# Order of the dt, q and z projections at the start of a block in a fused Mamba, attention and expert-FFN kernel

## The reference

```python
# layer 1, Mamba: DIN 1024 channels, N 16 states, R 32
x, z = split(layernorm(x0) @ in_proj_w)           # 512 -> 2 x 1024
xc = silu(conv4(x)); ssm = xc @ x_proj_w.T         # 1024 -> 32 + 16 + 16
dt = softplus(rmsnorm(ssm[:32]) @ dt_proj_w.T + dt_bias)
h[t] = exp(dt * A) * h[t-1] + dt * B[t] * xc       # a scan for each state
y = (sum_n h * C + D * xc) * silu(z); x1 = x0 + y @ out_proj_w.T
# layer 2, attention over ctx: 32 heads of 128, 8 key/value heads, rotary
q = layernorm(x1) @ Wq; k = ctx @ Wk; v = ctx @ Wv
x2 = x1 + softmax(mask(rope(q) rope(k).T / sqrt(128))) v @ Wo
# layer 3: a router picks 16 of 64 rank-8 experts
x3 = x2 + ffn(layernorm(x2))
```

## Time and profile before

| | us |
|---|---|
| median of 3 runs | 2348.61 |
| lowest, highest | 2341.81, 2349.77 |
| the profiled execution, its own time | 2350.73 |
| the span in its trace | 2349.1 |
| PE busy in it | 2086.0 |
| DVE busy in it | 1762.5 |
| ACT busy in it | 1003.9 |

### The profile page before, as it was taken

How to read it: one execution, slowest core, us unless ns; L and a number is a source line. 1 busy time by engine, 2 the same in 40 slices (tenths; PEclk the granted TensorE clock), 3 DMA queues, 4 the chain that set the end, 5 groups by cost and what they waited for, 6 DMA issues and landing times.

```text
span 2349.1 us, 26708 instructions
## 1 busy us (share of the span) xinstructions
PE 2086.0 (89%) x8268; PEld 1192.0 (51%) x8272; DVE 1762.5 (75%) x1735; ACT 1003.9 (43%) x2549; POOL 701.3 (30%) x492
## 2 busy tenths in 40 slices
PE   6877887898999988998999989998999989799988
PEld 2333454345555543445556544345556544477774
DVE  4499994459999996259999996259999994456553
ACT  2544440265555532155545541255545540233331
POOL 0289992401111112401111111501111110456550
PEclk9788999889999999989999999989999999799999
DMA  2579895527888873435888874525887874332210
GB/s 63 165 178 230 210 215 169 146 95 175 176 182 196 184 180 101 154 117 135 186 190 179 186 166 119 186 91 136 190 190 181 188 166 117 103 99 90 86 59 18
DMA packets 117810, 352.12 MB, mean 150 GB/s; under 512 B 14016, under 2 KB 14144, under 8 KB 115296
## 3 DMA queue, kind: packets, MB, share of 16 engines
q0 software_dynamic: 40704, 146.82, 32.3%
q1 hardware_dynamic: 70112, 191.68, 26.6%
q10 hardware_dynamic: 6912, 12.59, 1.4%
HBM read 197.68 MB, written 23.33 MB: 94 GB/s over the span
## 4 chain that ended last, share of the span: by engine, by line
DVE 34%; PE 27%; DMA 17%; issue 14%; ACT 3%; POOL 2%; DVEq 1%; PEldq 1%; SPq 0%; POOLq 0%; PEld 0%; ACTq 0%
DMA xc<-hs 15%; DVE hs L1254 11%; DVE hs L1431 4%; PE acc L1753 4%; PE acc L1631 3%; DVE hs L1261 3%; DVE hs L1245 2%; PE pq L1684 2%; PE acc L1837 2%; PE pq L1714 2%; PE pq L1921 2%; PE pk L1921 2%; PE acc L1766 1%; DVE pzsc L1311 1%; DVE qr L1291 1%
## 5 line engine op out<-in xcount | busy, mean ns | idle before, releaser
L768 POOL DMA_DIRECT2D xc<-hs x192 | 164.1, 860 | 1116.3 <-DVE hs L1261 1095.9
L1254 DVE TENSOR_TENSOR_SCAN hs<-dA,hs 128x1024 f32<-128x1024 f32 x192 | 428.7, 2274 | 0.0
L988 ACT ACTIVATE dA<-dt,aneg 128x504 f32<-128x504 f32 x384 | 253.6, 707 | 320.0 <-DVE hs L1254 319.8
L1684 PE MATMUL pq<-qT,wa 128*128 128x512 f32 x768 | 354.1, 615 | 15.1 <-DVE pzsc L1311 14.9
L1766 PE MATMUL acc<-wb,oT 128*128 128x512 f32 x768 | 352.2, 603 | 3.6 <-ACT oT L976 3.6
L1261 DVE TENSOR_TENSOR hs<-hs,bc 128x1024 f32<-128x1024 f32 x256 | 307.6, 1203 | 2.2
L953 ACT ACTIVATE pr<-pzsc,mx 128x64 f32<-128x64 f32 x512 | 170.8, 335 | 245.1 <-DVE mx L1317 245.1
L1245 DVE TENSOR_TENSOR hs<-u,bc 128x1024 f32<-128x1024 f32 x192 | 227.5, 1217 | 26.6 <-DMA xc<-hs 21.0
L1631 PE MATMUL acc<-xnT,wa 128*128 128x512 f32 x512 | 234.4, 612 | 14.3 <-DMA wa<-in_wx 3.9
L1684 PEld LDWEIGHTS pq<-qT,wa 128*128 128x128 f32 x768 | 146.4, 196 | 189.3 <-issue 177.2
L1766 PEld LDWEIGHTS acc<-wb,oT 128*128 128x128 f32 x768 | 141.2, 193 | 148.0 <-issue 143.9
(11 more groups left out here) (255 smaller groups left out, 3379.2 us busy)
## 6 DMA issues: line engine op xcount, KB each, us to landing
xc<-hs POOLq DMA_DIRECT2D x240, 512.0 KB, 7.0
bc<-bc_rows SPq DMA_DIRECT2D x64, 512.0 KB, 7.5
wa<-in_wq SPq DMA_DIRECT2D x64, 512.0 KB, 10.2
wb<-in_wo SPq DMA_DIRECT2D x64, 512.0 KB, 7.0
wa<-in_wx SPq DMA_DIRECT2D x16, 512.0 KB, 7.0
wa<-in_wz SPq DMA_DIRECT2D x16, 512.0 KB, 3.8
wb<-in_ow SPq DMA_DIRECT2D x16, 512.0 KB, 6.3
wv<-in_wv SPq DMA_DIRECT2D x26, 256.0 KB, 13.1
```

The costliest lines, as they stand in the source:

```text
L768: G.dma_start(xc[:, 2 * c:2 * c + 2, :], hs[:, c, :].rearrange("p (d t) -> p d t", t=T), accum_op=ALU.add).then_inc(s_y[c], 16)
L988: ins = S.activation(to[:, :, 1:SEQ], dt[:, s, :].rearrange("p (b t) -> p b t", t=SEQ)[:, :, 1:SEQ], ACT.Exp, scale=aneg[:, s, bass.ds(jj ...
L1254: V.tensor_tensor_scan(out=hs[:, c, :], data0=dA[:, c % 2, :], data1=hs[:, c, :], initial=0.0, op0=ALU.mult, op1=ALU.add).then_inc(scd.sem, 1)
L1684: ins = M.matmul(pq[:, h, :], wa4(p)[:, k, h * P:(h + 1) * P], qT[:, k, :], start=(k == 0), stop=(k == KE - 1))
```

## The change

It concerns the steady stages alone (`mamba and attn`).

- PE: dt is projected before q of pair 0. Of the four loads of z, z0 is projected between q 0 and scores 0, z1 between q 1 and step 0, and z2 and z3 (tiles 4 to 7) behind the whole of step 0, ahead of the zeros.
- ACT: exp and ln of softplus stand ahead of the exponentials of pair 0. Silu of z tiles 4 to 7 (`last_silu_z`) moves behind step 0.
- DVE: softplus chunk 0 stands between rope 0 and mask 0, chunk 1 between the maximum and the inverse sum of pair 0, chunks 2 and 3 behind rope 1. The wait for `y0r` ahead of step 0 goes.
- SP: the loads into `wa` follow PE's new order, q0, z0 | q1, z1, q2, z2, z3 | q3 ...; the loads z2 and z3 and q2 are issued behind those of xa, xr and xm. Step 0 issues no q load of its own.

```diff
@@ SP
-                    for n in range(2):
-                        load_wa(i, at_z + n, a["wz"][n])
+                    if attn:
+                        load_wa(i, 2, a["wq"][1])
+                        load_wa(i, 3, a["wz"][1])
...
+                if mamba and attn:
+                    load_wa(i, 4, a["wq"][2])
+                    for n in range(2, W_DT):
+                        load_wa(i, 3 + n, a["wz"][n])
...
@@ ACT
+                    if mamba and isinstance(jj, int) and jj == 0 and p == 0:
+                        last_silu_z()
...
@@ DVE
-                    for part in (mask_scores, max_scores, invert_sum, probs):
-                        part(0, 0)
+                    if mamba:
+                        softplus(i, ch, [0])
+                    mask_scores(0, 0)
+                    max_scores(0, 0)
+                    if mamba:
+                        softplus(i, ch, [1])
+                    invert_sum(0, 0)
+                    probs(0, 0)
                     rope_q(0, 1)
                 if mamba:
-                    softplus(i, ch)
+                    softplus(i, ch, [2, 3] if attn else range(NCH))
...
@@ PE
+                if attn:
+                    eng.wait_ge(qTr.sem, qTr.upto(blk, KE - 1))
+                    project_q(0, 0)
+                    free_wa(0, 0)
+                if mamba:
+                    eng.wait_ge(dtv.sem, dtv.upto(i, DT_TILES - 1))
+                if mamba and attn:
+                    project_z([0])
+                elif mamba:
+                    project_z(range(W_DT))
                 if attn:
                     scores(0, 0)
                     eng.wait_ge(srd.sem, srd.upto(blk, 0))
                     project_q(0, 1)
                     free_wa(0, 1)
...
+                if mamba and attn:
+                    project_z([1])
...
                     step(0, 0, False, first=True)
                     if mamba:
+                        project_z([2, 3])
                         eng.wait_ge(szr.sem, szr.upto(i, DT_TILES - 1))
```

More of the change, by code:

```diff
@@ L513, in one @@
                         eng.dma_start(bc[:, n, :, :], scr[i, :, n, :].partition_broadcast(P)).then_inc(s_bc[n], 16)
-                    for n in range(2):
-                        load_wa(i, at_z + n, a["wz"][n])
+                    if attn:
+                        load_wa(i, 2, a["wq"][1])
+                        load_wa(i, 3, a["wz"][1])
+                    else:
+                        for n in range(2):
+                            load_wa(i, at_z + n, a["wz"][n])
                     if attn:
@@ L586, in step @@
                         if not tail:
-                            load_wa_j(i, z_uses + 2, jj, p, a["wq"][jj * 2 + (2 + p)])
+                            if not (mamba and isinstance(jj, int) and jj == 0 and p == 0):
+                                load_wa_j(i, z_uses + 2, jj, p, a["wq"][jj * 2 + (2 + p)])
                             if p == 0 and mamba:
@@ L679, in one @@
                 if mamba:
-                    for n in range(2):
-                        load_wa(i + 1, n, a["wq"][n])
+                    load_wa(i + 1, 0, a["wq"][0])
+                    load_wa(i + 1, 1, a["wz"][0] if nxt else a["wq"][1])
                     load_wb(i + 1, 0, a["wo"][0])
@@ L1038, in one @@
                                      bias=chan[:, 1, s:s + 1]).then_inc(dtv.sem, 1)
-                if attn:
+                if attn and not mamba:
                     exps(0, 0)
-                    if not mamba:
-                        swap_q(0, 1)
+                    swap_q(0, 1)
                 if mamba:
@@ L1051, in one @@
                                      ACT.Ln, bias=1.0).then_inc(spl.sem, 1)
+                    if attn:
+                        exps(0, 0)
                     eng.wait_ge(yr.sem, yr.upto(i, -1))
@@ L1070, in one @@
                         S.activation(silu_z(s), acc[:, s % 4, :], ACT.Silu).then_inc(szr.sem, 1)
+                if mamba and not attn:
+                    last_silu_z()
                 def read_unit(at, what, b, g):
@@ L1219, in ssm_rows, with softplus @@
                                        op0=ALU.mult, op1=ALU.mult).then_inc(sstr.sem, 1)
-            def softplus(i, ch):
-                for c in range(NCH):
+            def softplus(i, ch, chunks):
+                for c in chunks:
                     two = slice(2 * c, 2 * c + 2)
@@ L1622, in wa4, with project_in @@
                 return wa[:, p, :].rearrange("p (k c) -> p k c", k=KE)
-            def project_in(b, loaded, banks, free, done):
-                for s in range(DT_TILES):
+            def project_in(b, loaded, banks, free, done, tiles=range(DT_TILES), slot=None):
+                for s in tiles:
                     if s % 2 == 0:
@@ L1629, in project_in @@
                     free(s)
+                    at = slot(s // 2) if slot else (s // 2) % 2
                     for k in range(KE):
-                        ins = M.matmul(banks(s % 4), wa4((s // 2) % 2)[:, k, (s % 2) * P:(s % 2 + 1) * P],
+                        ins = M.matmul(banks(s % 4), wa4(at)[:, k, (s % 2) * P:(s % 2 + 1) * P],
                                        xnT[:, k, :], start=(k == 0), stop=(k == KE - 1))
@@ L1679, in project_q @@
                         return
-                    z_loads = W_DT // 2 if o >= 2 else 0
-                    eng.wait_ge(s_wa[p], (wa_half(i) + (o // 2 + 1 + z_loads) + jj) * 16)
+                    if isinstance(jj, int) and jj == 0:
+                        at = [0, 2, 4, 7][o]
+                        p = at % 2
+                        use_wa(at)
+                    else:
+                        eng.wait_ge(s_wa[p], (wa_half(i) + (o // 2 + 1 + W_DT // 2) + jj) * 16)
                     for h in range(2):
@@ L1838, in one, with free_z, project_z @@
                                  stop=True).then_inc(dtd.sem, 1)
+                def free_z(s):
+                    if s >= 4:
+                        eng.wait_ge(szr.sem, szr.upto(i, s - 4))
+                def project_z(loads):
+                    place = [1, 3, 5, 6] if attn else [at_z + n for n in range(W_DT)]
+                    project_in(i, lambda n: use_wa(place[n]), lambda b: acc[:, b, :], free_z, inz,
+                               range(2 * loads[0], 2 * loads[-1] + 2), lambda n: place[n] % 2)
+                if attn:
+                    eng.wait_ge(qTr.sem, qTr.upto(blk, KE - 1))
[5 more added lines that the diff above has]
+                    project_z([0])
+                elif mamba:
+                    project_z(range(W_DT))
                 if attn:
```

11 lines of the change are left out of this document (1 added, 10 removed).

## The result

| | before | after |
|---|---|---|
| median, us | 2345.58 (4 runs) | 2365.41 (4 runs) |
| lowest, highest | 2341.81, 2349.77 | 2363.02, 2368.13 |
| ratio, 95% interval | | 1.0084, [1.006, 1.0109] |
| span in the trace | 2349.1 | 2363.4 |

The changed kernel is slower by 19.8 us. The chain that ended last, by engine (part 4 of the page of the changed kernel), answers to the earlier trace rows: PE now leads it and DVE follows.

A forecast was written before the change was run, and what follows sets the result against it. DVE is full once step 0 runs, but PE is the nearer limit at mask 2: 10.7 us later less 1.9 given back is 8.8 per stage, 26.4 over three, 2348.61 to 2375 us; 8-in-10 range 2350 to 2391.

The forecast's parts named there:

- dt first: On PE ahead of q 0: 1.9 us lost waiting for ssmT, then dt itself takes 10.5 us.
- The clock: On PE behind dt: q 0 slow at 9.7 us, q 1 7.1, scores 0 at full clock, a gain of 2.9.
- The gain on DVE: On DVE up to mask 1: softplus moved into the waits brings mask 1 7.6 us earlier.
- PE's gap and z behind q 2: On PE before mask 2: 13.9 us without work but values, then q 2, z2, z3; DVE idle some 18 us.
- The load of z3: On SP's queue behind q 2: landing takes 10.2 us, low end 3.8, so z3 lands 2.9 us late for PE.
- B's part: Rival, costs come out low: z3 lands within 3.8 us, q 0 at full clock, q 2 at 8.7; 2355, chance 0.15.
- The mask behind the scores: On DVE at mask 2: the mask starts 0.7 us after scores 2 end on PE.
- silu and zeros: Behind z3: four silus on ACT take 2.07 us uncovered, then PE's four zeros take 1.1 us.
- Given back: On DVE in the step behind mask 2: a 1.9 us wait for an accumulating DMA falls away.
- Rival C: Faster: the 7.6 us that DVE is early at mask 1 carry through mask 2; 2326 at full gain, chance 0.11.
- D: Rival, heavier: q 2 at half clock throughout, 14.1 us not 9.7, another 4.4 per stage; 2388, chance 0.12.

The follow-up runs named there:

- q_first: The changed kernel with q of pair 0 ahead of dt on PE again, all else as changed: 2362.09 us, ratio 1.0085 to the kernel before.
- warm_gap_long: The changed kernel with products of zeros in PE's gap, 24 ahead of values 0 and 25 behind: 2363.1 us, ratio 1.0077 to the kernel before.
- z_ahead: The changed kernel with z2 and z3, their silus and loads, back ahead of step 0: 2333.21 us, ratio 0.9958 to the kernel before.
- z_in_gap: The changed kernel with z2 and z3 between scores 1 and values 0, last silus behind evac_o: 2340.68 us, ratio 0.9993 to the kernel before.
- warm_gap: The changed kernel with products of zeros in PE's gap, 24 ahead of values 0 and 16 behind: 2362.59 us, ratio 1.0093 to the kernel before.

## Why the prediction was right

The direction, the place and nearly the size came out: 26.4 us were forecast, 19.8 measured. The walk of the prediction against the trace, second steady stage, in us after ssmT:

| step | forecast | measured |
|---|---|---|
| q 0 starts (dt done) | 10.6 | 13.4 |
| q 0 takes | 9.7 | 9.2 |
| mask 0 | 32.5 | 34.5 |
| mask 1 (before 72.9) | 65.3 | 67.7 |
| q 2 takes | 9.7 | 9.0 |
| wait of z3 for its load | 3.2 | 0.4 |
| zeros start | 95.6 | 94.6 |
| mask 2 (before 94.2) | 105.0 | 103.2 |

*dt first.* The 1.9 us of wait were there (1.83) in the second and third stage. dt itself was taken at its old 10.5 and took 13.46, 11.47 in the third stage and 8.19 in the first, where it did not wait. In the second PE now idles right before it, where q 0 stood: between 998 and 1012 the granted clock is 0.55, against 0.68 over the dt stretch of before (1002 to 1013), and with q 0 ahead again (q_first) dt took 10.41. This term was too small by up to 3 us.

```profile
998.00:1012.00 14.00, 13.24 (x16) 4.87 (x16) 0.71 (x1) 8.86 (x14) 0.00 (x0) 0.55 0.25 80
```

*The clock.* q 0 took 9.24 to 9.53, so the forecast from the row of the slow q was right. q 1 was forecast at full clock, 7.1, and took that in the second stage only; in the first and third it took 8.61 and 8.74. The Trainium skill's sentence that activity releases the throttle (TensorE: Matmul & The Clock Gate, "What's actually happening"), read so that dt counts as activity, would have put q 0 at 7.03 and been wrong by 2.2 us here. The same section of the Trainium skill gives the low clock to an idle TensorE, and with that the trace agrees: the granted clock was 0.50 in the gap, q 2 behind it was slow, and warm_gap_long took that away.

*The gain on DVE.* Forecast 7.6 us at mask 1, measured 5.2; the difference is dt.

*PE's gap and z behind q 2.* This is the mechanism, and the experiment on it (z_ahead) came within 4 us of the time expected for it. The gap before q 2 was forecast as 13.9 us and is 7.15 + 5.08 idle with 2.08 of values; the wait at mask 2, forecast as some 18, is 13.94 to 14.11.

*The load of z3.* This is the term that was mis-sized most. I took 10.2 us from issue to landing, the median of wq. The trace of the changed kernel has this load, issued at 1076.36, landed after 5.1 us, and those of the other two stages after 3.4 and 3.3:

```profile
wa<-in_wz SPq DMA_DIRECT2D x1, 512.0 KB, 5.1
```

z3 starts at 1084.04 with 0.39 idle, not for a DMA; forecast were 3.2. B's part on this was right, as the prediction had said it would show. The thirteen wq loads issued behind it in this stage, from 1083 to 1357 us, took 9.8 to 10.6 us; each is issued about 1 us behind a B and C row load of 512 KB, where the z3 load is the first of its group on SP's queue. That fits queueing as the reason for the long median, which no run here isolates.

*The mask behind the scores.* The prediction adds 0.7 us between the last score and its mask. Its own rows give 0.25 (1019.48 + 0.63 to 1020.36), and from turn_probs 1 to mask 2, forecast as 8.3, the trace has 7.75.

*silu and zeros.* Forecast 2.1 for the silus; PE waits 2.16.

*Given back.* Forecast 1.9 per stage. The steps behind mask 2 in the second stage brought the shift from 9.0 down to 6.7 (the last mask 389.1 after ssmT, 382.4 before); in the first stage from 4.1 to 3.6, and in the third it grew from 9.5 to 9.7. So 2.6 us in all and not 5.7. In the second stage the 1.88 us wait behind mask 2 is gone, as forecast. Together 20.0 are left at the last masks, close to the 19.8 of the medians. In the one traced execution of each kernel the spans differ by only 14.3. Most of the rest went behind the steps: in the first stage a wait for a wx load is 1.10 us where it was 2.46, and the way from the last z-gating to ssmT took 116.7 us for 118.5. That the change causes this is not shown; z_ahead's trace varies there as well.

*The sum.* At mask 2 three times 10.7, that is 32.1 us, were forecast, and 22.6 measured. By term: from mask 1 to mask 2 the three stages grew by 42.4 us and not by 54.9. Of these 12.5 us some 8.5 are the wait of z3, 2.1 q 2 (8.84, 9.01 and 9.17 for 9.7) and 1.6 the step from scores to mask. Against that, mask 1 came 19.8 us sooner in all and not 22.8, and behind mask 2 there were 3.1 us less given back. 12.5 - 3.0 - 3.1 = 6.4, the distance from 26.4 to the 20.0 of the last masks. So the near hit owes something to errors that offset each other.

*The first stage* lost only 4.1 at mask 2, the others 9.0 and 9.5. There ssmT is ready before v is through, so dt starts without a wait and takes 8.19, and mask 1 gains 9.8 us, where the others gain 5.2 and 4.8. I had used the second stage for all three; the 7.6 us forecast for each lie between.

Rival C fell: DVE did come early to mask 1, but none of it passed mask 2. D fell: q 2 took 9, not 14.

## What to carry to other kernels

When work is spread so that one engine opens a loop earlier, look up what its first wait inside the loop is for, and add up the other engine's queue up to that point; here 14.2 us of projection had been placed behind the very product that waits for the faster engine, and the whole gain turned into a wait. Put movable work into the slower engine's gap ahead of such a point, or leave it ahead of the loop: keeping only the part that fills DVE's waits (softplus between the softmax parts) makes this kernel 0.4% faster than before. And every moved instruction has a place in its engine's in-order queue: the silus, two table loads with them, took back part of what z_in_gap could have gained by standing ahead of `normalise`.

## What the runs showed of the hardware

- TensorE busy nearly all the time is not TensorE at full clock. The dt products (32 rows) kept PE busy for 13.24 of 14 us at a granted clock of 0.55, and the q behind it took 9.24 for 7.13.
- With products of zeros in bf16 in the gap (warm_gap, second stage) the granted clock was 1.00, the 2.4 GHz level, from 1053 to 1067 us; in the changed kernel it was 0.50 from 1056 on. q 2 took 7.13 wherever at most 0.78 us were left idle before it, and 8.83 behind 1.96 and 2.43. The idle time right before a product does not settle it alone: behind 1.10 and 0.97 us of it, q 1 of the changed kernel took 8.61, 7.13 and 8.74.
- How long a load of 512 KB takes to land depends on where it is issued: 3.3 to 5.1 us for the z3 load, first of its group on SP's queue, and 9.8 to 10.6 for the wq loads of the same stage issued behind another load.
